# The order of look and scores in the first cross attention of a two-layer perceiver

## The reference, cut to what matters

```python
x = x + xattn(layernorm(x), ctx)          # x: 16 x 64 x 256, ctx: 16 x 1601 x 192
# xattn:
q = (x @ wq + bq).reshape(B, 64, 16, 16)
k = (y @ wk + bk).reshape(B, 1601, 16, 16)
v = (y @ wv + bv).reshape(B, 1601, 16, 16)
scores = einsum('bqhd,bkhd->bhqk', q, k) / sqrt(16)
attn = softmax(scores, axis=-1)
out = einsum('bhqk,bkhd->bqhd', attn, v).reshape(B, 64, 256)
return out @ wo + bo
```

## Time and profile before

| | |
|---|---|
| median of 3 runs | 1844.58 us (1842.8 to 1854.05) |
| profiled execution | 1846.77 us |
| its span | 1845.0 us |
| TensorE busy | 1783.5 us, 97% |
| VectorE busy | 1339.7 us, 73% |
| ScalarE busy | 1009.2 us, 55% |
| GpSimd busy | 938.4 us, 51% |
| chain that ended last | TensorE 79%, VectorE 9%, ScalarE 6% |

### The profile page before, as it was taken

How to read it: one execution, slowest core, us unless ns; L and a number is a source line. 1 busy time by engine, 2 the same in 40 slices (tenths; PEclk the granted TensorE clock), 3 DMA queues, 4 the chain that set the end, 5 groups by cost and what they waited for, 6 DMA issues and landing times.

```text
span 1845.0 us, 44731 instructions
## 1 busy us (share of the span) xinstructions
PE 1783.5 (97%) x17870; PEld 1555.4 (84%) x17870; DVE 1339.7 (73%) x2790; ACT 1009.2 (55%) x2138; POOL 938.4 (51%) x1178
## 2 busy tenths in 40 slices
PE   7999999999999999999999999999999999989998
PEld 6888888888878778889999999999999986657887
DVE  6888888878888967667676767666666745757775
ACT  5677676766767735454444444444444434526664
POOL 3787777777787427355433334333333312514553
PEclk9999999999999999999999999999999999999999
DMA  6121111211110110133222222222323007051111
GB/s 164 38 73 38 38 38 38 72 39 38 38 38 2 60 50 1 61 93 107 64 63 63 63 63 63 63 63 63 87 72 85 8 5 297 1 194 23 32 32 16
DMA packets 50750, 113.11 MB, mean 61 GB/s; under 512 B 4928, under 2 KB 37264, under 8 KB 49008
## 3 DMA queue, kind: packets, MB, share of 16 engines
q1 hardware_dynamic: 46128, 105.13, 19.1%
q0 software_dynamic: 4416, 5.12, 1.6%
HBM read 105.78 MB, written 5.37 MB: 60 GB/s over the span
## 4 chain that ended last, share of the span: by engine, by line
PE 79%; DVE 9%; ACT 6%; issue 3%; DMA 1%; POOL 0%; SPq 0%; DVEq 0%; POOLq 0%; ACTq 0%
PE ps L104 8%; PE ps L166 8%; PE ps L514 5%; PE ps L495 5%; PE ps L1781 5%; PE ps L472 4%; PE ps L2756 3%; PE ps L489 3%; PE ps L1782 2%; PE ps L424 2%; DVE arena L1893 2%; PE ps L1768 2%; PE ps L1770 2%; PE ps L1767 2%; PE ps L1771 2%
## 5 line engine op out<-in xcount | busy, mean ns | idle before, releaser
L617 DVE TENSOR_REDUCE arena<-ps 128x1 f32<-128x400 f32 (+1 forms) x512 | 258.0, 566 | 87.6 <-PE ps L472 87.2
L777 ACT ACTIVATE arena<-ps 128x384 f32<-128x384 f32 (+1 forms) x512 | 223.3, 524 | 94.8 <-PE ps L495 93.6
L1781 PE MATMUL ps<-arenaR 128*128 128x386 f32 x768 | 242.0, 373 | 1.1 <-DVE arenaR L1887 1.1
L878 POOL TENSOR_TENSOR arena<-arena 128x512 f32<-128x512 f32 (+1 forms) x152 | 197.1, 1297 | 77.1 <-ACT arena L777 68.8
L1997 ACT CAST arenaR<-ps 128x512 fp32r<-128x512 f32 (+1 forms) x256 | 116.8, 508 | 200.5 <-PE ps L166 199.6
L1782 PE MATMUL ps<-arenaR 128*128 128x194 f32 x768 | 193.8, 252 | 0.0
L1887 DVE TENSOR_TENSOR arenaR<-ps,arenaR 128x512 fp32r<-128x512 f32 (+1 forms) x256 | 138.9, 585 | 28.9 <-ACT arenaR L1997 28.9
L2022 ACT ACTIVATE wsb<-ps,arena 128x1200 f32<-128x1200 f32 x64 | 81.0, 1265 | 131.4 <-DVE arena L1946 131.4
L1782 PEld LDWEIGHTS ps<-arenaR 128*128 128x128 f32 x768 | 146.9, 191 | 0.0
L1781 PEld LDWEIGHTS ps<-arenaR 128*128 128x128 f32 x768 | 145.0, 189 | 1.4 <-DVE arenaR L1887 1.4
L1893 DVE TENSOR_REDUCE arena<-ps 128x1 f32<-128x400 f32 (+1 forms) x256 | 137.1, 566 | 0.6 <-PE ps L1771 0.6
(11 more groups left out here) (384 smaller groups left out, 5089.6 us busy)
## 6 DMA issues: line engine op xcount, KB each, us to landing
wsb<-in_ctx SPq DMA_DIRECT2D x16, 1152.0 KB
wsb<-in_ctxT SPq DMA_DIRECT2D x16, 800.5 KB, 4.8
wsb<-in_ctxT SPq DMA_DIRECT2D x32, 400.2 KB, 7.4
gu<-in_m_gu SPq DMA_DIRECT2D x8, 1536.0 KB, 18.9
arena<-in_ctxT SPq DMA_DIRECT2D x15, 800.5 KB, 5.2
arena<-in_ctxT SPq DMA_DIRECT2D x30, 400.2 KB, 7.3
dn<-in_m_dn SPq DMA_DIRECT2D x8, 768.0 KB, 11.3
wsb<-in_f_w SPq DMA_DIRECT2D x2, 1024.0 KB, 5.9
```

What stands on the lines that cost most here:

```text
L617: e.tensor_reduce(mx4[n % 2][:, u, i:i + 1], ps[:, at("look", n, i, u), 0:400 + (i == 3)], AX.X, ALU.max).then_inc(c.maxed.at((n, i, u)), 1)
L777: e.activation(v[:, u, 0:128 * GN[s]], ps[:, at("st", n, s, u), 0:128 * GN[s]], ACT.Exp).then_inc(c.exp_a.at((x0, n, s, u)), 1)
L878: e.tensor_tensor(sums_p[0:k], sums_p[0:k], v[0:k, :, 128 * t:128 * t + 128], ALU.add).then_inc(added_p.at((n, s)), 1)
L1781: e.matmul(o, PTh[:, t, :], v[:, t, 0:386], start=(t == 0), stop=False)
```

## The change

In each half of a round the look stands ahead of the scores, in the table of banks and in TensorE's list. The lists of the other engines stay as they are.

```diff
@@ -329,11 +329,11 @@
     at("v", 0, 6)
     for r in range(LAST + 1):
         for i in range(2):
+            for use in looks(r)[i:i + 1]:
+                at_look(*use)
             for n, s in groups(r)[i:i + 1]:
                 for u in range(4):
                     at("st", n, s, u)
-            for use in looks(r)[i:i + 1]:
-                at_look(*use)
             if r >= 1 and i == late(r):
                 at("sum", r - 1)
         for use in keys_of(r)[:1]:
@@ -565,10 +565,10 @@
         vals(0, 6)
         for r in range(LAST + 1):
             for i in range(2):
+                for use in looks(r)[i:i + 1]:
+                    look_at(*use)
                 for use in groups(r)[i:i + 1]:
                     scores(*use)
-                for use in looks(r)[i:i + 1]:
-                    look_at(*use)
                 if r >= 1 and i == late(r):
                     values(r - 1)
             for use in keys_of(r)[:1]:
```

## The result

The changed kernel takes 1899.57 us, median of 4 runs (1897.67 to 1900.54), against 1844.93 us before (4 runs, 1842.8 to 1854.05). The ratio is 1.0284, 95% interval 1.0266 to 1.0303, so 49 to 56 us more. The forecast was 1906.

What follows compares the result with a forecast made beforehand. TensorE was taken to set the pace, busy 478.52 of 484 us in the first cross attention. Profiled 1846.8 plus 62 (odd rounds 44, even rounds 18) minus 2.2 to the median gave 1906 us, range 1870 to 1930.

Steps and rivals of the forecast that it cites:

- Banks and chain: Each round: keys take the second look's first bank, behind look, scores, four exps, additions and one VectorE maximum.
- Odd round: Rounds with three key tiles in both scores: keys at 6.77 us against 5.29, +1.48 in each of 30.
- Who goes first: Even rounds: whether VectorE's or GpSimd's addition is ahead after one exp; left open, +0.2 or +1.05 us a round.
- the middle value of 0.6: Even rounds: +0.6 us each, taken between +0.2 and +1.05; 30 rounds give 18 us.
- Rival C: GpSimd's addition goes first in even rounds: 30 by 1.48 and 30 by 1.05, 76 us, 1921; chance 0.24.
- the +1.05 of the prediction: Even rounds with GpSimd's addition ahead: VectorE's takes 1.77 us, keys at 6.73, +1.05 us a round.
- the +0.2 of the right order: Even rounds with VectorE's addition ahead: it takes 0.68 us, only the second scores' late bank is left, +0.2 us a round.
- Steps costed at nothing, or nearly: First look's keys' copy, GpSimd's queries and value sums' bank: no wait; release of the last values' bank: 0.03 us.
- Sum: Rounds 0 to 59: 30 odd by 1.48 is 44, 30 even by 0.6 is 18, +62 us, to 1906.
- A: VectorE's and GpSimd's additions do not meet: 30 by 0.37 and 30 by 0.2, 17 us, 1862; chance 0.09.
- B: Not slower: first maxima start sooner, the chain ends ahead of 5.3 us and nothing waits, 1842; chance 0.04.
- D: TensorE's clock falls in the gaps of the rounds, 58 us on top, 1964; chance 0.03.

Runs made afterwards that it cites:

- the two half changes: Against the kernel before, look ahead of scores in the first half of a round only, 1864.27 us, or in the second half only, 1888.55 us.

## Why the prediction was right, step by step

**Banks and chain.** Right. The keys are released by VectorE's maximum in 29 waits, and the two half changes show the place: the second half, where the keys get the look's bank, carries most of it, with the first half's late exps on top.

**Odd round.** Predicted keys at 6.77, +1.48; measured 6.65, +1.36. Link by link: scores at 0.84 for 0.72 (the look's own 0.69 was right, as rounds 18, 26 and 34 start their scores at 0.67 to 0.68; the rest is the last values' copy, which runs from 0.11 to 0.69 in the round shown, with the scores 0.15 behind its end), exps to 3.72 for 3.63, additions at 3.75 for 3.70, their step 2.29 for 2.43, maximum and release 0.61 for 0.64. The step came from a single row, in which GpSimd's addition had begun first, by 0.03, and VectorE's two took 2.52; here VectorE's begins first, and they take 2.37. 30 rounds gave 39.7 for 44 us. The first maxima, put at about 0.9, start at 1.10, which costs nothing, since VectorE waits for the exps behind them.

**Who goes first.** Open in the prediction, and the term that was mis-sized. In every even round from 2 to 58 VectorE's addition starts ahead of GpSimd's, by 0.04 to 0.14 (once 0.30), and keeps its 0.69 to 0.88. So the middle value of 0.6 was too high: 29 rounds gave 8.1 us for 18, 0.28 on average. Rival C (GpSimd first) is out; where that order occurs, in the experiment with the look first in the second half only, it costs 0.63 to 0.83, for the +1.05 of the prediction. That 0.28 lies near the +0.2 of the right order is in part luck. Of the 8.1 us, 4.0 lie in the six rounds 8, 16, 24 and so on to 48, where the scores wait 0.41 to 0.46 for a copy of ScalarE's (L754, in round 8 L781), and 2.6 in rounds 52 to 58; both stand mostly behind waits in front of the scores that the sum did not have. The other nineteen lose 0.08 on average: round 4 gains 0.47, the rest lose 0.04 to 0.27.

**Steps costed at nothing, or nearly.** Two were wrong. I gave the release of the last values' bank 0.03 where odd rounds show 0.15, and did not count the queries' bank at all. Waits of the scores for L754, L611 and L1271 are 6.4 us in sum after; before, the look waited 0.5 us once for such a bank (L611, round 52), and no other wait of this kind passes 0.15 us. They are inside the 8.1 us of even rounds and in odd rounds 53, 55 and 57, which lose 1.56. The keys' copy for the first look, GpSimd's queries and the value sums' bank cost nothing, bar one wait of 1.1 us (L514).

**Sum.** The span grew by 50.8 us, for the 62 of the sum; 44 + 18 against 39.7 + 8.1. Between the medians there are 54.6 us, within the interval of 49 to 56. Both terms were too large, so the forecast did not come out by errors that cancel; 1899.57 lies 6 us below it.

**The other rivals.** A (no meeting of VectorE and GpSimd) is refuted in the changed kernel, and made true by the experiment in which GpSimd waits: it was put at 1862 and came at 1867.9. B fell with the result, and the clock of D stayed full from 60 to 585 us. The Trainium skill's rule (SBUF — State Buffer, Who interferes with whom), that such a pair of instructions shuts each other out, agrees with these runs: 2.37 us for two additions beside a GpSimd addition, 1.42 without, 2.15 for three.

## What to carry to other kernels

Where banks go round in the order of use, moving a step changes which engine frees the bank of every later step: write down, for each use, who frees the bank before it and what stands ahead of that on its engine. A consumer's bank freed by an engine that first has to do work depending on a third engine is the costly case. And before an addition is split between VectorE and GpSimd, ask whether both halves start from one releaser in front of something that TensorE waits for; one wait on the half that nobody needs was worth 32 us here (1899.57 to 1867.92).

## What the runs showed of the hardware that I had not expected

Released by the same exp, VectorE's addition starts 0.04 to 0.10 us ahead of GpSimd's in nearly all rounds, and its first addition keeps its full speed (0.69) while GpSimd's is stretched from 1.27 to 1.72 or 1.78. Where GpSimd's has begun 0.01 to 0.05 us sooner, in the experiment on the second half, VectorE's can take 1.80 and GpSimd's 1.27, or VectorE's 0.68 and GpSimd's 1.82: start times that near do not tell which one goes first. A wait of TensorE of 1.3 us in every second round, some 7% of the time, left its granted clock at 1.00 from 60 to 585 us.
